# Context and base weight stored piece by piece: one contiguous run per partition for each load

## The reference

```python
# stage A
q1 = fake_quant(layernorm(x), x1_scale, x1_zp)        # 0..255 integers, then (q - z) * s
q2 = fake_quant(ctx_4096, x2_scale, x2_zp)
x = x + tanh(g_xattn[0]) * matmul(q1, q2)
# stage B
h = layernorm(x)
base = einsum('bsd,od->bso', h, base_W)
w = top-2 of softmax(h @ router_W.T), renormalised, over 8 experts
inc = sum over experts e of (h @ lora_A[e] * w[e]) @ lora_B[e]
x = x + tanh(g_ffn[0]) * (base + 2 * inc)
```

## Time and profile before

| | us |
|---|---|
| time, median of 3 runs | 1163.68 |
| lowest, highest of the 3 | 1163.39, 1164.04 |
| span of the profiled execution (the one time that it has) | 1164.5 |

### The profile page before, as it was taken

One profiled execution on the slowest core, in us unless ns is written; L12 is line 12 of the kernel. 1 busy time (PEld: TensorE's weight loads), 2 busy tenths in 40 slices (PEclk: granted clock), 3 DMA queues, 4 the chain that ended last, 5 costly groups with the idle time before them and its releaser, 6 DMA issues.

```text
span 1164.5 us, 13520 instructions
## 1 busy us (share of the span) xinstructions
PE 1085.9 (93%) x5130; PEld 816.5 (70%) x5152; DVE 594.8 (51%) x876; ACT 297.2 (26%) x291; POOL 189.4 (16%) x123
## 2 busy tenths in 40 slices
PE   1678987989999999998999999989999999999998
PEld 1333433334688888887888887878888789888887
DVE  7999698976763543343237224334533343222231
ACT  6642344310241212231112113111211321111210
POOL 3766678662300000000000000000000000000000
PEclk9999998999999999999999999999999999999999
DMA  9885997647572633507242633351542614162440
GB/s 361 299 298 179 311 327 224 236 147 256 190 262 67 200 116 105 194 23 291 73 153 70 211 99 118 132 212 55 181 144 73 199 40 142 54 203 84 148 145 37
DMA packets 111051, 193.88 MB, mean 166 GB/s; under 512 B 30608, under 2 KB 32656, under 8 KB 106896
## 3 DMA queue, kind: packets, MB, share of 16 engines
q1 hardware_dynamic: 68368, 153.18, 38.1%
q10 hardware_dynamic: 42624, 39.85, 11.0%
HBM read 153.16 MB, written 33.55 MB: 160 GB/s over the span
## 4 chain that ended last, share of the span: by engine, by line
PE 71%; DVE 10%; issue 6%; POOL 6%; DMA 4%; ACT 1%; SPq 1%; ACTq 0%; DVEq 0%; POOLq 0%
PE acc L818 17%; PE acc L820 17%; PE acc L819 17%; PE acc L795 3%; POOL ctx_quant L380 3%; PE acc_even L818 3%; PE acc_even L819 3%; PE acc_even L820 3%; DMA w_stage<-in_wt 2%; DVE bn_chunks L540 2%; DVE ctx_tree_sums L591 2%; PE aT_psum L855 1%; PE aT_psum L856 1%; POOL x_group_odd L394 1%; PE aT_psum L833 1%
## 5 line engine op out<-in xcount | busy, mean ns | idle before, releaser
L818 PE MATMUL acc<-w_hi,hT_hi 128*128 128x512 f32 x896 | 353.8, 395 | 0.0
L820 PE MATMUL acc<-w_hi,hT_lo 128*128 128x512 f32 x896 | 350.3, 391 | 0.0
L819 PE MATMUL acc<-w_lo,hT_hi 128*128 128x512 f32 x896 | 349.9, 390 | 0.0
L667 DVE TENSOR_TENSOR w_lo<-w_stage,w_hi 128x1024 fp32r<-128x1024 f32 x128 | 156.6, 1224 | 320.7 <-ACT w_hi L476 318.6
L476 ACT ACTIVATE w_hi<-w_stage 128x1024 fp32r<-128x1024 f32 x128 | 135.6, 1059 | 460.3 <-PE acc L820 314.2
L820 PEld LDWEIGHTS acc<-w_hi,hT_lo 128*128 128x128 f32 x896 | 168.8, 188 | 35.9
L819 PEld LDWEIGHTS acc<-w_lo,hT_hi 128*128 128x128 f32 x896 | 169.0, 189 | 34.2
L818 PEld LDWEIGHTS acc<-w_hi,hT_hi 128*128 128x128 f32 x896 | 168.8, 188 | 33.9
L795 PE MATMUL acc<-ctx_quant,aT_even 128*128 128x512 bf16 x501 | 121.2, 401 | 10.4 <-DVE x_group_even L611 7.9
L795 PE MATMUL acc<-ctx_quant,aT_odd 128*128 128x512 bf16 x501 | 113.7, 383 | 5.0 <-DVE x_group_odd L611 4.4
L795 PEld LDWEIGHTS acc<-ctx_quant,aT_even 128*128 128x128 bf16 x512 | 52.0, 103 | 77.5 <-issue 21.8
(11 more groups left out here) (129 smaller groups left out, 1011.8 us busy)
## 6 DMA issues: line engine op xcount, KB each, us to landing
w_stage<-in_wt SPq DMA_DIRECT2D x128, 512.0 KB, 5.8
ctx_stage<-in_ctx SPq DMA_DIRECT2D x32, 1024.0 KB, 6.5
x_group_even<-x_scratch SPq DMA_DIRECT2D x16, 1024.0 KB, 10.4
residual<-x_scratch SPq DMA_DIRECT2D x64, 256.0 KB, 4.0
out<-residual ACTq DMA_DIRECT2D x64, 256.0 KB, 2.8
x_group_even<-in_x SPq DMA_DIRECT2D x8, 1024.0 KB, 9.0
x_group_odd<-in_x SPq DMA_DIRECT2D x8, 1024.0 KB, 8.1
x_scratch<-x_group_even ACTq DMA_DIRECT2D x8, 1024.0 KB, 4.9
```

The source lines that it names most:

```text
L667: dve.tensor_tensor(wl[s][:, :], wst[s][:, :], wh[s][:, :].bitcast(F32), ALU.subtract)\
L818: pe.matmul(out_, lh, rh, start=first, stop=False)
L819: pe.matmul(out_, lh, rl, start=False, stop=False)
L820: return pe.matmul(out_, ll, rh, start=False, stop=final)
```

## The change

The two inputs are laid out in HBM in the order of their pieces. A context piece is 128 rows of 2048 floats, one row per partition, and a weight piece 128 rows of 1024 floats. Each load then reads one run of 8 KB (context) or 4 KB (weight) per partition, and the whole piece is one contiguous stretch of HBM. The bytes, the buffers, the number of loads, their order on SP and what they wait for are the same; the data in a buffer is the same too. No instruction moves on any engine. The loads of x, of `x1_scratch` and of the LoRA inputs, and all stores, are as they were.

```diff
         def w_piece(X):
             Y = X % WG
-            k0, n = WK * (Y % WP), Y // WP
-            return wt[k0 * P:(k0 + WK) * P, n * NW:(n + 1) * NW].rearrange("(k p) n -> p k n", p=P)
+            return wt[Y * P:(Y + 1) * P, :]
...
-                src = ctx[b, p * PK * P:(p + 1) * PK * P, n * NW:(n + 1) * NW]
-                sp.dma_start(cst[q % CS][:, :, :], src.rearrange("(k p) n -> p k n", p=P))\
+                row = ((b * NB + n) * CP + p) * P
+                sp.dma_start(cst[q % CS][:, :, :].rearrange("p k n -> p (k n)"), ctx[row:row + P, :])\
                     .then_inc(c_in[q % CS], 16)
...
             def load_w(X):
-                sp.dma_start(wst[X % RING][:, :].rearrange("p (k n) -> p k n", n=NW), w_piece(X))\
-                    .then_inc(w_in[X % RING], 16)
+                sp.dma_start(wst[X % RING][:, :], w_piece(X)).then_inc(w_in[X % RING], 16)
...
+    ctx_pieces = np.asarray(ctx_4096).reshape(2, CP, PK, P, NB, NW).transpose(0, 4, 1, 3, 2, 5)
+    w_pieces = np.asarray(L0_ffn_base_W).T.reshape(WP, WK, P, NB, NW).transpose(3, 0, 2, 1, 4)
     arrays = {
...
-        "in_ctx": np.asarray(ctx_4096),
-        "in_wt": np.asarray(L0_ffn_base_W).T,
+        "in_ctx": ctx_pieces.reshape(2 * NB * CP * P, PK * NW),
+        "in_wt": w_pieces.reshape(NB * WP * P, WK * NW),
```

## The result

| | before | after |
|---|---|---|
| median of 20 runs each, us | 1164.08 | 1168.31 |
| lowest, highest | 1160.92, 1169.16 | 1164.45, 1171.67 |
| ratio after to before, 95% interval | | 1.0029 [1.0018, 1.0041] |
| span of the profiled execution, us | 1164.5 | 1165.9 |

The change makes the kernel slower by 0.29%, some 3.4 us by the ratio. The forecast was 1163.2 with a range up to 1164.8: the time lies outside it, and on the other side of the time before. Single runs of one kernel lie up to 5 us from their median here; the three runs shown before the prediction lay within 0.65 us of each other by chance. One run of the kernel before, beside e1 to e4, took 2461 us and stands in no ratio.

A forecast was written before the change was run, and what follows sets the result against it. The prediction took PE and DVE as full from 40 to 300 us and PE in stage B, with DMA mattering only where an engine waits. Gains of 0.2 (start), 0 and 0.3 (stage B) gave 1163.68 - 0.5 = 1163.2 us, range 1161.2 to 1164.8.

The forecast's parts named there:

- the stage B term: Last column block of three groups: the weight load PE waits behind lands 0.1 us sooner each, 0.3 us less in all.
- Rival A, faster: Stage B: contiguous runs close the 2.2 us gap from last residual to first weight load to 1.25; 1161.1 us, chance 0.15.
- Rival B, slower: Stage A: longer packets delay ACT's transposes by up to 2.5 us; two places at 1.5 us, +3, 1166.7 us; chance 0.08.
- The mark for it at 181 us: ACT's transpose at 181 us holds it some 4.9 us as before; 6 or more would mean Rival B.
- The start: DVE's 0.56 us wait for the second x tile: it lands 0.2 us sooner behind one context piece, 0.2 us less.
- The context load at 52 us: A context load with nothing ahead of it takes 4.8 us instead of 5.0.
- The 30 other context loads: Rest of stage A: they land some tenths sooner, but nobody waits for those pieces; worth 0.
- The packet counts: Whole kernel: 82,379 packets instead of 111,051, of them 74,128 under 8 KB, the bytes the same.
- 125 of 128 weight loads: Stage B: the ring of four buffers keeps them ahead of PE, so their being faster is worth 0.
- The price c of a packet: DMA loads: a fixed 8 ns per packet beside a part per KB, saving a weight piece 0.07 us.
- Stage A's +-0.7 us: Stage A: allowance for which DVE and POOL instructions fall beside each other, estimated from the size of the shifts.
- The base and the range: Profiled execution, 1164.5 us, taken as 0.8 above the run median, 1163.68; range holding 8 in 10, 1161.2 to 1164.8.

The follow-up runs named there:

- e1: Kernel before with only the context laid out by pieces (8 KB runs), weight loads as before; ratio to before 0.9999 [0.9983, 1.0014].
- e4: The kernel after, unchanged, run once more beside other kernels; ratio to before 1.0031 [1.0011, 1.0051].
- e11: Kernel before with context load 26 held until ACT comes to a stage A transpose, so that they meet; ratio to before 1.0004 [0.9990, 1.0019].
- e2: Kernel before with only the weight laid out by pieces (4 KB runs), context as before; ratio to before 1.0015 [0.9999, 1.0031].
- e3: Kernel after with each dense piece ordered (k, p, n), so loads have 2 KB runs again; ratio to before 1.0039 [1.0022, 1.0055].
- e7: Kernel after with context loads 24 and 27 held until the DMA transpose beside them has landed; ratio to before 1.0013 [0.9999, 1.0026].
- e13: Kernel before with only the weight laid out by pieces, e2 taken again in another set; ratio to before 1.0020 [1.0004, 1.0035].
- e5: Kernel after with a column block's first three weight loads issued ahead of the store wait and residual loads; ratio to before 0.9977 [0.9961, 0.9993].
- e6: Kernel before with a column block's first three weight loads issued ahead of the store wait and residual loads; ratio to before 0.9965 [0.9953, 0.9978].
- e9: Kernel before with context loads held beside transposes and weight loads issued ahead of the residual; ratio to before 0.9964 [0.9950, 0.9979], median 1161.47 us.
- e14: Dense pieces with 2 KB runs (e3), context loads held and weight loads ahead of the residual; ratio to before 0.9979 [0.9969, 0.9989], median 1162.64 us.
- e12: Kernel after with each weight row followed by 1024 unused floats: 4 KB runs at 8 KB pitch, not dense; ratio to before 1.0059 [1.0036, 1.0081].

## Why the prediction was wrong

**The step that failed** is the stage B term: "The residual loads and stores are not changed. Three times 0.1 us is 0.3." Their instructions aren't changed; their landing is. The sum over all executions with PE's waits in place:

| weights | executions | last residual load, mean | first weight load, mean | PE waits, sum |
|---|---|---|---|---|
| old | before, e1, e11 | 6.7 | 8.7 | 3.0, 1.2, 2.4: mean 2.2 |
| dense | after, e2, e3, e4, e7, e13 | 8.3 | 9.6 | 5.8, 3.7, 5.9, 4.7, 4.9, 5.0: mean 5.0 |

The term was -0.3 us and measures +2.8. Stage B in all is 858.0 us on the mean of the old three (858.3, 857.4, 858.2), and 861.4 on that of the dense six (859.6 to 862.8): 0.6 us of the difference lies beside the waits. That the waits are the cause, and not a companion, is shown by e5, where they are gone and the loss with them. Why a residual load lands 1.6 us later when dense weight loads are queued behind it, I can't say. It isn't the number or length of packets (e3), and it isn't the context (e1). In the last group's last column block the effect is missing (5.8 us after, 6.5 before), and in the middle column blocks it is mostly missing (once 8.2 us in e2 and 8.1 in e4, but also once 8.2 in e6 and 8.1 in e9 with the old layout). One thing sets the three places apart in all executions, of either layout: a packet of 16 KB on the queue of instructions, 0.9 to 1.0 us on one DMA engine, starts within 0.2 us of the first residual load's issue. It is this one in after, from 471.8 to 473 us (queue, packets, MB, share of 16 engines):

```profile
q8 instruction: 1, 0.02, 4.6%
```

No middle block has it at that time. But the last group has it too, 0.8 us ahead to 0.1 us behind, and lands no later than 7.4 us, so by itself it isn't enough, and no run leaves it out. A weight load held back until the residual loads have landed would test it further; it wasn't tried.

**Rival A, faster, had the right gap and the wrong end of it.** It took the 2.2 us between the last residual load and the first weight load for a price of scattered runs, and said that it would close to 1.25. It closed, to 1.30 in each of the three groups. But the landing in front moved back by more than the gap lost: the rival held "697.6" fixed, as the forecast did.

**Rival B, slower,** named a transpose held up behind a longer load, at "two such places at 1.5 us". The event is there, one transpose and 18.0 us instead of 6.0. Its mechanism, long packets of the context, isn't needed: e3 has it with 2 KB runs. The mark for it at 181 us was put one transpose too late: ACT's transpose moved from there to 183.50 and holds ACT 3.4 us. And its price was hidden for the most part. The kernel is slower, but not by this rival.

**What held.** The start: x tile 1 lands at 11.06 instead of 11.49, and DVE's timeline has the wait at 0.30 instead of 0.56:

```profile
11.09 2.47 DVE L538 BATCH_NORM_STATS2 bn_chunks<-x_group_even 128x6 f32<-128x512 f32 x4 [0.30 <-DMA x_group_even<-in_x]
```

0.26 us of the wait and 0.42 of the start time, where 0.2 was taken (0.17 of it because the first x tile was early as well). The context load at 52 us takes 4.9 us where it took 5.0 (4.8 to 5.1 in the other executions with 8 KB runs, 5.1 to 5.8 with the old context, but 6.2 and 7.4 in e3 and e14, dense with 2 KB runs), forecast 4.8. The 30 other context loads are worth 0: e1 is 0.9999. The packet counts. And 125 of 128 weight loads worth nothing, by e5 beside e6. The price c of a packet, 8 ns, is right too: on SP's queue the median packet takes 84 ns for 2 KB, 159 for 4 KB and 309 for 8 KB, so two packets of 2 KB cost 9 ns more than one of 4 KB.

**What was too small.** Two weight loads with nothing beside them, at 554 and 559 us, first of before, then of after:

```profile
DMA to landing us min/median/max: 3.8/3.9/3.9
```
```profile
DMA to landing us min/median/max: 3.1/3.1/3.2
```

That is 0.75 us less for 512 KB where 8 ns a packet gave 0.07. It changed nothing in the sum, since the load isn't alone where it counts. Nor is it the packets for the most part. Over the 31 to 33 weight loads of an execution that have no other load beside them the median is 3.8 us in before, 3.45 in e3 (dense, 2 KB runs), 3.7 in e12 (4 KB runs, not dense) and 3.2 in after: dense pieces give 0.36 to 0.48 us, longer runs 0.11 to 0.23. The forecast's model of a load, a fixed part and bytes, has no term for where a piece lies, and this is the term that it lacked at both ends: dense loads land sooner alone, and the load in front of them later. By the Trainium skill (DMA: Bandwidth & Descriptors, "Why small descriptors are slow (HBM only)") a packet costs a fixed 3 cycles beside one per 32 bytes, which makes an estimate of 3 of 67 cycles, 4.5%, of a 2 KB packet. The traces here have more, 9 of 84 ns, 11%.

**Stage A's +-0.7 us.** The forecast put this on "which instructions of DVE and POOL fall beside each other". The one DVE instruction of 1.95 or 0.22 us alone is 1.7 us, against the kernel before. It makes the two profiled executions look closer than the kernels are: their spans differ by 1.4 us, the medians of 20 runs by 4.2. Whether it comes with the program or by chance is open: of the four executions with both inputs in the old layout, before and e6 have it, e9 and e11 don't, and e1, with the new context, has it.

**The base and the range.** The forecast put the profiled execution 0.8 us above the median by its span. In every later execution that has both numbers the time is 1.8 to 2.1 us above the span (after: 1167.86 and 1165.9). If before is like them, its profiled execution took 1166.4 us, 2.7 above the median of three. With single runs that far apart, a range that ended 1.1 us above that median was too narrow even for the kernel unchanged: its own median is 1164.08 in 20 runs, and 1164.83 to 1165.56 in the four sets beside the experiments, each above the range's end. The time of the kernel after, 1168.3, lies beyond these too.

## What to carry to other kernels

When a transfer is made cheaper, ask which other transfers stand in the same queue around the one place where an engine waits, and give each of them a term with two bounds, also those that the edit doesn't touch. A load that an engine waits for belongs ahead of loads that nobody needs yet; here that order was worth 4 us with the old layout (e6) and some 6 with the new (e5 beside after). And subtract PE's wait from the landing that releases it in a few places: if the difference is constant, the path is proved, and only the landing is left to explain.

## What the hardware did that I had not expected

- Two transfers on one queue act on each other backwards: a 256 KB residual load lands 8.3 instead of 6.7 us after the first one's issue, when the 512 KB loads that are issued behind it read dense pieces. The packets of the residual load are the same. It is so in the last column block of the first three groups, and mostly not in the others.
- A DMA transpose that lands in 4.2 to 5.4 us alone, and in 10 to 13 us with one or two loads issued into it, sometimes takes 17 to 22, and the loads beside it 15 to 20, while the DMA engines stay busy and move 113 GB/s instead of 301; in its issue ACT is held 1.3 to 2.1 us alone and up to 6.9 beside loads.
- One DVE instruction of 128x1 takes 1.95 us in some executions and 0.22 in others, with POOL's next instruction starting 0.05 us behind it in both.
- Dense pieces or not, 2, 4 or 8 KB runs: with PE's waits gone the intervals of all the ratios overlap (0.9964 to 0.9979).
